# Decoder layer pair on one core: self attention's scores in three groups on four row tiles, operand loads in shares between contexts, latent turns one slot behind

## The reference

```python
# 1. self attention: 4 branches x 16 heads of 16, keys shared by the branches
q, v = rope(X @ Wq + bq), X @ Wv + bv          # 64 heads of 16
k = rope(X @ Wk + bk), tiled over the branches
w = softplus(q @ k.T * 16**-0.5 / |k|); w = where(causal, w, 0)
w = w * sigmoid(pi/sqrt(3) * w)
out = (w @ v + sink * v_null) / (sum(w) + sink)  # then @ Wo, mean over branches
...
# 2. cross attention over ctx_1024: 16 heads of 16, plain softmax over 361 keys
...
# 5. latent attention: 16 heads of 64, queries from X, 361 + 100 keys from layer-normed [ctx_1024, X]
sim = (ln(X) @ Wq) * scale @ (kv_in @ Wkv)[k].T ; softmax ; @ v ; @ Wout ; layer norm
```

## Time and profile before

| what | value |
|---|---|
| median of 3 runs | 2532.61 us (2527.84 to 2534.07) |
| the profiled execution's own time | 2523.02 us |
| its span in the profile | 2521.4 us |
| PE busy | 2123.3 us (84%) |
| DVE busy | 1353.3 us (54%) |
| ACT busy | 1126.2 us (45%) |
| POOL busy | 473.7 us (19%) |
| granted TensorE clock, mean of the span | 0.917 |
| self attention, first to last PE work | about 39 to 549 us |
| cross attention | about 553 to 998 us |
| latent attention | about 1321 to 2248 us |

### The profile page before, as it was taken

How to read it: one execution, slowest core, us unless ns; L and a number is a source line. 1 busy time by engine, 2 the same in 40 slices (tenths; PEclk the granted TensorE clock), 3 DMA queues, 4 the chain that set the end, 5 groups by cost and what they waited for, 6 DMA issues and landing times. The chain is left out here.

```text
span 2521.4 us, 48525 instructions
## 1 busy us (share of the span) xinstructions
PE 2123.3 (84%) x17362; PEld 1312.1 (52%) x17363; DVE 1353.3 (54%) x3264; ACT 1126.2 (45%) x2404; POOL 473.7 (19%) x533
## 2 busy tenths in 40 slices
PE   1899899865999997867768999999999999864992
PEld 0455555543666664644434555555555555552661
DVE  1677777742555555368873555555555555521223
ACT  0566666632555553235553454444444544420110
POOL 2565555400000001134430000000000000003002
PEclk9799999866999998879989999999999999966996
DMA  5000000024000000000000000000000000035101
GB/s 155 1 2 0 0 0 0 2 60 136 19 18 12 18 12 1 1 1 0 0 6 12 7 7 6 6 12 6 6 6 6 6 7 6 1 106 202 34 29 58
DMA packets 50461, 60.82 MB, mean 24 GB/s; under 512 B 9849, under 2 KB 44974, under 8 KB 49918
## 3 DMA queue, kind: packets, MB, share of 16 engines
q1 hardware_dynamic: 47366, 53.74, 6.9%
q0 software_dynamic: 3008, 5.91, 0.8%
HBM read 51.11 MB, written 8.52 MB: 24 GB/s over the span
## 5 line engine op out<-in xcount | busy, mean ns | idle before, releaser
L2156 DVE CUSTOM_DVE_ANT_0 la_pr<-la_pS,la_mb 100x461 f32<-100x461 f32 x256 | 148.1, 636 | 195.5 <-PE la_pS L2019 195.5
L2001 PE MATMUL la_side<-la_wkv,la_inT 128*128 128x512 f32 (+1 forms) x512 | 242.5, 596 | 0.0
L2257 ACT ACTIVATE la_pr<-la_pr,la_nm 100x461 f32<-100x461 f32 x256 | 171.9, 674 | 134.9 <-DVE la_nm L2156 134.9
L1989 PE MATMUL la_side<-la_inT,la_wkv 128*128 128x461 f32 x512 | 227.3, 566 | 1.3 <-ACT la_inT L2241 0.8
L2265 ACT COPY la_pT<-la_pPT 128x400 f32<-128x400 f32 x256 | 126.1, 493 | 165.4 <-PE la_pPT L2027 164.2
L2027 PEld LDWEIGHTS la_pPT<-io_ident,la_pr 100*128 100x128 f32 x1024 | 110.4, 144 | 148.9 <-issue 105.6
L1029 DVE TENSOR_REDUCE ca_nm<-ca_pS 100x2 f32<-100x722 f32 x128 | 116.1, 907 | 111.7 <-PE ca_pS L916 109.8
L2324 POOL TENSOR_TENSOR la_xb<-io_X,la_bo 100x256 f32<-100x256 f32 x16 | 11.6, 725 | 838.6 <-DVE io_X L2145 838.6
L2027 PE MATMUL la_pPT<-io_ident,la_pr 100*128 100x100 f32 x1024 | 137.6, 258 | 29.7 <-ACT la_pT L2265 18.4
L1101 ACT ACTIVATE ca_pr<-ca_pS,ca_nm 100x361 f32<-100x361 f32 x256 | 129.8, 560 | 64.3 <-DVE ca_nm L1029 62.5
L2118 DVE COPY la_v<-la_side 128x512 f32<-128x512 f32 (+1 forms) x128 | 87.7, 686 | 101.2 <-PE la_side L2001 101.2
(11 more groups left out here) (356 smaller groups left out, 4359.2 us busy)
## 6 DMA issues: line engine op xcount, KB each, us to landing
rf_w<-in_L_ffn_W SPq DMA_DIRECT2D x16, 1024.0 KB, 14.4
ca_cn<-in_ctx SPq DMA_DIRECT2D x16, 256.0 KB, 2.7
la_cn<-in_ctx SPq DMA_DIRECT2D x16, 256.0 KB, 2.8
rows_in<-io_zero SPq DMA_DIRECT2D x20, 128.0 KB, 4.7
rb_xr<-rows_in POOLq DMA_DIRECT2D x20, 128.0 KB, 2.3
rows_out<-rb_yr SPq DMA_DIRECT2D x20, 128.0 KB, 1.7
ea_wcT<-in_t_L_ffn_conv_W SPq DMA_DIRECT2D x1, 2048.0 KB
la_wkv<-in_L_xattn_Wkv SPq DMA_DIRECT2D x1, 2048.0 KB
```

Source lines behind the costliest of these rows:

```text
L1989: last = nc.tensor.matmul(pf[:, 0:SK], wkv[:, k, e * P:(e + 1) * P], inT[:, k, :], start=k == 0, stop=k == KD - 1)
L2001: last = nc.tensor.matmul(pf[0:keys[c], :], inT[:, k, c * P:c * P + keys[c]], wkv[:, k, o:o + 512], start=k == 0, stop=k == KD - 1)
L2156: ins = nc.vector.tensor_tensor_reduce(out=pr[m % 2][:, e, 0:SK], in0=pS[0:T, 2 * (m % 2) + e, 0:SK], in1=mb[b][:, :], scale=-1.0, scalar= ...
L2257: ins = nc.scalar.activation(pr[m % 2][:, e, 0:SK], pr[m % 2][:, e, 0:SK], ACT.Exp, scale=-1.0, bias=nm[m % 2][:, e:e + 1], accum_out=zs[m ...
```

## The change

Self attention: the scores come in three groups n = 0, 1, 2 in place of six chunks. A group uses all four row tiles and all four banks, and waits until the whole group before has been read. DVE's masking stays in six pieces but stands in pairs; `softplus` part 0 moves behind `xT_read`, and the orders of all three streams change around it. Cross attention: the operand loads (31 now, with the first latent context's memory moved in) are issued three behind each context's load, from context 1 on. Latent attention: turns of a slot are made in the next slot (`pr` has four buffers), `values` two slots later, ORDER is re-laid so that a turn stands behind every step, the inputs of two contexts ahead are worked on from slot 1 on, and in the last context the turns alternate between `pPT` and a free side bank. The setup of `mb`, `v` and `pr` moves behind the first inputs.

```diff
     def load(self, sp):
-        with self.st.nc.allow_non_contiguous_dma("small constants"):
...
+        for t, src in self.pairs:
+            self.one(sp, t, src)
...
-                def scores(s, b, c):
-                    if c == 0:
+                def scores(s, b, n):
+                    if n == 0:
                         pe.wait_ge(s_kT, s + 1)
                         pe.wait_ge(s_qT, s + 1)
-                    above(pe, s_sm, s * NCH + (c - 1))
-                    for g in range(KD) if c < 2 else (c // 2 - 1,):
-                        for e in range(2):
-                            j = 2 * (c % 2) + e
+                    above(pe, s_sm, s * NCH + 2 * n)
+                    for g in range(KD) if n == 0 else (n - 1,):
+                        for j in range(NJ):
                             tile = slice(QR * j, QR * (j + 1))
...
-                    dv.wait_ge(s_S, s * NCH + (c + 1))
+                    dv.wait_ge(s_S, s * NPT + (c // 2 + 1))
...
                     if F:
                         k_biased(f)
+                    if S:
+                        masked(s, 1)
                     if O:
                         context_read(o)
-                    if S:
-                        masked(s, 1)
...
-                    if S:
-                        softplus(s, par, 0)
                     if V:
                         normalised(v, 3)
                     if N:
                         xT_read(f + 1, par)
                     if S:
+                        softplus(s, par, 0)
                         softplus(s, par, 1)
                         softplus(s, par, 2)
...
-                load(0)
-                for x in later:
-                    x.load(sp)
-                for i in range(1, 3):
+                todo = [(x, t, src) for x in later for t, src in x.pairs]
+                share = -(-len(todo) // (NB - 4))
+                for i in range(NB):
                     load(i)
-                with sp.Fori(3, NB) as i:
-                    load(i)
+                    if i:
+                        for x, t, src in todo[(i - 1) * share:i * share]:
+                            x.one(sp, t, src)
...
-    ORDER = [["by", "fk0", "fv00", "fk1", "fv01"], ["fk2", "fv10", "fk3", "fv11", "fq0"],
-             ["fk4", "fv20", "fk5", "fv21", "fq1"], ["fk6", "fv30", "fk7", "fv31", "gl", "gc0", "gc1"]]
+    ORDER = [["fk0", "fk1", "fk2", "fq0", "fk3"], ["by", "fv00", "fk4", "fv01", "fk5"],
+             ["fv10", "fk6", "fv11", "fk7", "fv20"], ["fq1", "fv21", "fv30", "fv31", "gl", "gc0", "gc1"]]
...
-        pr = [sb(f"pr{b}", [T, 2, KP_]) for b in range(2)]
+        pr = [sb(f"pr{b}", [T, 2, KP_]) for b in range(4)]
...
+                    if over:
+                        pe.wait_ge(s_PT, max(2 * n + e - 1, 2 * NB * MP - 2 * MP - 4))
+                        pe.wait_ge(s_R[spare.bank], spare.before)
+                    else:
+                        above(pe, s_PT, 2 * n + e)
+                    dst = side[spare.bank] if over and e else pPT
...
-                        if j:
-                            both_values(i, b, j - 1)
+                        if j > 1:
+                            both_values(i, b, j - 2)
...
+                        for h in range(4):
+                            some(h + 1)
+                            if j:
+                                turn(i * MP + 2 * j - 2 + h // 2, 2 * j - 2 + h // 2, h % 2, final)
...
-                        exps(i, 2 * j)
-                        some(2)
-                        exps(i, 2 * j + 1)
                         for h in range(4):
-                            if h:
-                                some(2 + h)
-                            evac(i * MP + 2 * j + h // 2, h // 2, h % 2)
+                            some(h + 1)
+                            if j:
+                                evac(i * MP + 2 * j - 2 + h // 2, h // 2, h % 2, final)
...
+                            if h < 2:
+                                exps(i, 2 * j + h)
```

More of the change, by code:

```diff
@@ L81, in want, with one @@
         return t
+    def one(self, sp, t, src):
+        with self.st.nc.allow_non_contiguous_dma("small constants"):
+            dst = t[0:src.shape[0]] if len(t.shape) == len(src.shape) else t[:].rearrange("p a b -> p (a b)")
+            sp.dma_start(dst, src).then_inc(self.s_in, 16)
     def load(self, sp):
-        with self.st.nc.allow_non_contiguous_dma("small constants"):
-            for t, src in self.pairs:
-                dst = t[0:src.shape[0]] if len(t.shape) == len(src.shape) else t[:].rearrange("p a b -> p (a b)")
-                sp.dma_start(dst, src).then_inc(self.s_in, 16)
+        for t, src in self.pairs:
+            self.one(sp, t, src)
     def wait(self, eng):
@@ L659, in body @@
                         sigmoid(s, par, 0)
+                        sigmoid(s, par, 1)
                     if V:
@@ L1861, in at @@
         if isinstance(i, int):
-            gone = len(self.g) if i == NB - 1 else 0
-            return self.At(self.lead + self.per * i + k - gone, None, self.per)
+            back = next(q for q, n in enumerate(self.names) if n[0] == "b")
+            if i == 0:
+                k += k < back
+            elif i == NB - 1:
+                k -= len(self.g) + back
+            return self.At(self.lead + self.per * i + k, None, self.per)
         return self.At(self.lead + k, i, self.per)
@@ L1949, in latent_attention @@
         turns = Banks(ORDER)
+        spare = turns.last()
         with nc.Block() as block:
@@ L1959, in load @@
                     sp.dma_start(cn[0:ckeys[2], 2, :], d["ctx_1024"][i, 2 * P:SC, :]).then_inc(s_cn, 16)
-                for i in range(3):
+                for i in range(1, 3):
                     load(i)
@@ L2059, in body @@
                                 step(name, n, i + turns.AHEAD[name[0]], turns.buffer(name, b))
-                            turn(i * MP + 2 * j + h // 2, h // 2, h % 2)
-                        for _, name, n in todo:
-                            step(name, n, i + turns.AHEAD[name[0]], turns.buffer(name, b))
+                        for h in range(4):
+                            some(h + 1)
+                            if j:
+                                turn(i * MP + 2 * j - 2 + h // 2, 2 * j - 2 + h // 2, h % 2, final)
+                            elif not first:
+                                turn(i * MP - 2 + h // 2, MP - 2 + h // 2, h % 2, final)
+                        some(9)
                 w.wait(pe)
@@ L2067, in _ @@
                 over_batches(pe, body, 3)
+                both_values(NB - 1, 1, MD - 2)
+                for h in range(4):
+                    turn(NB * MP - 2 + h // 2, MP - 2 + h // 2, h % 2, True)
                 both_values(NB - 1, 1, MD - 1)
@@ L2202, in _ @@
                 nc.vector.memset(cmv[:], 1.0).then_inc(s_e, 1)
-                for b in range(2):
-                    ch.after(nc.vector.memset(mb[b][:], 0.0))
                 dv.wait_ge(s_e, 1)
@@ L2207, in _ @@
                 apply_inputs(0)
+                for b in range(2):
+                    ch.after(nc.vector.memset(mb[b][:], 0.0))
                 mask(0, 0)
-                dv.wait_ge(s_z, 4)
+                dv.wait_ge(s_z, 6)
                 for name, j, n in turns.prologue():
@@ L2308, in _ @@
                         inputs(1)
-                ac.wait_ge(s_z, 4)
+                ac.wait_ge(s_z, 6)
                 over_batches(ac, body, 3)
+                sums(NB - 1, 1, MD - 2)
+                for h in range(4):
+                    evac(NB * MP - 2 + h // 2, h // 2, h % 2, True)
                 sums(NB - 1, 1, MD - 1)
@@ L2327, in _ @@
                 stage(0)
+                po.wait_ge(s_n, 1)
                 for b in range(2):
                     nc.gpsimd.memset(v[b][:, NC - 1, :], 0.0).then_inc(s_z, 1)
+                for b in range(4):
                     nc.gpsimd.memset(pr[b][:], 0.0).then_inc(s_z, 1)
                 stage(1)
+                stage(2)
                 residual(0)
-                stage(2)
-                residual(1)
-                with po.Fori(2, NB - 1) as i:
-                    stage(i + 1)
+                with po.Fori(1, NB - 2) as i:
+                    stage(i + 2)
                     residual(i)
+                residual(NB - 2)
                 residual(NB - 1)
```

111 lines of the change are left out of this document (52 added, 59 removed).

## The result

| | median | runs |
|---|---|---|
| before | 2531.63 us | 2527.84 to 2534.07 (4) |
| after | 2447.11 us | 2444.26 to 2449.74 (4) |

What follows compares the result with a forecast made beforehand. PE is full in latent attention, slowed by clock and waits in self attention, stopped 25.40 us for memory in cross attention. Terms -29 + 0 - 20 = -49 from 2532.6 give 2484 us; range 2455 to 2508.

Steps and rivals of the forecast that it cites:

- Part 1, operand loads: Cross attention: loads issued behind each context's load no longer delay the second context's memory; -29 us, bounds -20 and -31.
- The hole's 24.8: Cross attention: PE's 25.40 us standstill for the second context's memory goes, less 0.6 us; -24.8 us.
- The shadow of -4: Cross attention: steps behind the hole, run at the lower clock, return to the full clock; -4 us, bounds 0 and -5.8.
- Part 2, self attention: Self attention: PE saves 2.3 us a pass, but DVE's later context reading takes it back; sum 0.
- I take 0, bounds -10 and +12: Self attention: spells at the lower clock may cost less each but become more numerous; net 0 us.
- The sign that the prediction gave: Self attention: the prediction is wrong if the stage's mean clock leaves 0.85 to 0.97.
- Its remark that a spell beside a wait costs less: Self attention: spells fall at a pass's beginning, where PE will wait some 2 us anyway, so one costs less.
- The first rival: Self attention: DVE catches up, the context reading is not late, and 30 us are gained; 2454, chance 0.15.
- DVE's lateness arrives in full: Self attention: the late context costs its full time, or low-clock spells come in every pass; +20, 2504, chance 0.17.
- The slower rival: Self attention: PE's idle stretches keep the clock at 0.50 for 60% of a pass; +75, 2560, chance 0.03.
- Part 3, latent attention: Latent attention: waits go at its start, first slot, steady part and last context; -20 us, bounds -10 and -31.
- 1.57 us of waiting goes: Latent attention, first slot: no turn stands in it, so PE's waiting there goes; 1.57 us.

Runs made afterwards that it cites:

- only_sa: The kernel before with the self attention part of the change alone (three score groups on four row tiles, new orders on all engines); 2493.77 us, ratio 0.9854.
- ctx_earliest: The changed kernel with DVE's context reading back ahead of the second masking and of the first softplus part, as before the change; 2423.96 us, ratio 0.9582.
- halves: The changed kernel with each group of self attention scores issued as two halves one after the other, two row tiles each; 2490.62 us, ratio 0.9851.
- group_twice: The kernel before with only the scores grouped in three on four row tiles, each group issued twice; 2496.14 us, ratio 0.9865.
- group_only: The kernel before with self attention's scores in three groups on four row tiles and nothing else moved; 2477.34 us, ratio 0.9801.
- twice: The changed kernel with each group of self attention scores issued twice on all four row tiles; 2478.01 us, ratio 0.9803.

## Why the prediction was wrong

**Part 1, operand loads: right.** Forecast -29, bounds -20 and -31; alone it measures -24.2, and the stage is 25.6 us shorter in the trace of the whole. Over all runs the stage takes 426 to 434 us with the old loads (nine traces, mean 428.7) and 399 to 407 with the shares (six, mean 403.2). The hole's 24.8 is there. The shadow of -4 is not: after the change the first steps run at the lower clock themselves (0.88 in the first window above). The loads ahead of the second context's memory were 29 in the trace, not 30.

**Part 2, self attention: the step that failed is "I take 0, bounds -10 and +12"** for the spells at the lower clock. The mechanism of the pass was right: `out_projected` comes 9.02 us behind the last turn of the values (193.47 to 202.49) instead of 7.60 (314.11 to 321.71), 1.42 us late where the prediction said 1.5; the pass is 27.20 us where it said near 27; the wait it named is 2.30 us. But the stage had 54 us at 1.2 GHz, which the prediction itself had read, and it treated these as weather that a change of PE's order could only make worse. They were a cost of the old order. Five or six long spells became three short ones, 20 to 26 us; the first passes are some 5 us shorter, the steady ones cost 0.3 each: -21 to -28 for the stage. The clock's share lies outside its bound of -10, the stage within the part's -30. The sign that the prediction gave, a mean clock above 0.97, was at its edge (0.98 to 440 us, 0.97 to 480). Its remark that a spell beside a wait costs less held: two of the three short ones cost nothing. The whole part measures -37.5; the trace of only_sa shows 25.2 of that in the stage and some 5 in the unchanged ones behind it, and the rest is not attributed.

**The first rival** (scores' time arrives, 2454) comes near in time and is wrong in its reason. DVE was late; ctx_earliest shows what it would have been without that. "DVE's lateness arrives in full" was the wrong way round too: it arrived, and was hidden under a larger gain. The Trainium skill, TensorEngine Tiling (Array Packing), section Performance Considerations, says that tiling speeds up TensorE but not the reading of PSUM, which may then become the limit. The trace agrees only in part: what DVE reads from PSUM did come late, but 4.82 us of what stood ahead of it are softplus parts that read no PSUM, against 0.76 and 0.75 us for the two maskings that do.

**The slower rival** was right to name the clock and wrong in its sign. PE idles more now (82% busy against 90%) and the clock is higher. Idle time alone is no measure for it. The Trainium skill, TensorE: Matmul & The Clock Gate, section on a second HAM failure mode, puts such a clock down to idle times between groups of matmuls; here the short falls do lie behind waits (in halves behind the 2.0 us for the context), but the kernel with less idle time had the longer ones. Its sum was also mixed: 34.9 us has 60% of a pass's work at the lower level, which is 75% of the time, and was set beside 18% of the time.

**Part 3, latent attention: mechanism right, size small.** Forecast -20, bounds -10 and -31; alone -28.1, in the trace -24.0. Start -2.8 (forecast -2.7). Last context -11.0 (forecast -11), a number met partly by luck: the waits named are gone and a slot takes 8.1 to 8.6 us without `by` (forecast 7.2 to 8.5), but the higher clock of this execution is in it, and in the run with the latent part alone it is -9.5. The middle contexts take 54.64 us instead of 55.01, thirteen of them -4.8 (forecast -5). The mis-sized term is the first slot, "1.57 us of waiting goes": the first context is 4.5 us shorter, since its first slot has no turns and no values at all. They move to the last context, where the prediction had added them (4 us) without taking them off here. The next to last context gives 1.3 more.

**The sum.** Of the 35.5 us missed, self attention in its stage is 21 to 28, the unchanged stages 6, latent attention 4 to 8; cross attention gave 4 less. The 9.6 us by which the profiled execution of before lay under the median went into the forecast unchanged. Most of that offset lies in the first stage: its first projection of cross attention came at 558.7 us, in the runs with the same first stage at 565.5 and 567.5. One long spell fewer is 4.4 us of it.

## What to carry to other kernels

Read a mean clock below 1 as a cost of the stage with a place: find where in a pass the spells begin and what PE does in them, before putting a change of PE's order at zero. Then give every change of order its price on each engine apart: here the new grouping on PE was worth 54 us, the new orders around it took 16 of them back, and two steps of DVE's order alone were worth 21 to 23, which no total shows. And a part that looks like nothing should be run alone, with the offset of the profiled execution from the median explained and not carried along.

## What the runs showed of the hardware

A stage whose code no edit touches changed by 5 us with the stages before it. In the kernel before, DVE was idle for 2.6 us ahead of one instruction (`ea_hn`) and waited for nothing the profile shows, in only_sa for 2.2 us; PE's idle time before the next matmul was 1.76 and 1.37 us, and behind the longer one the clock fell. From the first `ea_wcT` matmul to the last turn of the bucketed attention there are 283 to 285 us in all six runs with 2.6, and 279 to 280 in eight of the nine with 2.2 (group_twice has 284). That the 0.4 us cause it is argued from the place, not shown.

More work went with a higher clock once and not the other time. group_twice issues every score matmul twice and has no fall in its steady passes, where group_only has four; it is still slower by 18.8 us, as a pass takes 27.2 instead of 25.83 us. The same doubling in the changed kernel (twice) took the falls from three to eight.
